# A graph-network kernel's edge MLP: stacked edge attributes, two weight parts side by side, a second addition, and masked register loads

## The reference

```python
edge_input = jnp.concatenate([x[src], x[dst], edge_attr, u[batch[src]]], axis=-1)
h = jax.nn.relu(edge_input @ W1 + b1)
agg = jax.ops.segment_sum(h, dst, num_segments=x.shape[0])
new_input = jnp.concatenate([x, agg, u[batch]], axis=1)
return jax.nn.relu(new_input @ W2 + b2)
```

## Time and profile before

| | us |
|---|---|
| median of 3 executions | 6733.62 |
| lowest, highest | 6725.39, 6737.43 |
| span of the profiled execution | 7388.9 |

### The profile page before, as it was taken

One profiled execution on the slowest core, in us unless ns is written; L12 is line 12 of the kernel. 1 busy time (PEld: TensorE's weight loads), 2 busy tenths in 40 slices (PEclk: granted clock), 3 DMA queues, 4 the chain that ended last, 5 costly groups with the idle time before them and its releaser, 6 DMA issues.

```text
span 7388.9 us, 160613 instructions
## 1 busy us (share of the span) xinstructions
PE 5124.8 (69%) x52214; PEld 4234.4 (57%) x52215; DVE 3236.4 (44%) x5886; ACT 1321.7 (18%) x3390; POOL 2130.6 (29%) x3521
## 2 busy tenths in 40 slices
PE   1999988777777799892655565655565567747665
PEld 1777776666666699892555554554554553323265
DVE  7999888777777611213222222222222231030133
ACT  0122234455555400000000000000000000010010
POOL 1222222222222100002555555555555540000000
PEclk9999999999999989995555555555555558979977
DMA  1011223334343388875222222222222228969755
GB/s 33 24 51 55 79 75 103 131 122 137 123 140 126 117 327 350 341 283 97 60 59 56 60 59 57 59 59 56 59 59 56 60 55 330 418 249 418 319 232 210
DMA packets 427400, 1053.65 MB, mean 143 GB/s; under 512 B 126711, under 2 KB 283713, under 8 KB 398401
## 3 DMA queue, kind: packets, MB, share of 16 engines
q1 hardware_dynamic: 377090, 1000.81, 38.0%
q0 software_dynamic: 50176, 51.48, 3.3%
HBM read 809.69 MB, written 242.41 MB: 142 GB/s over the span
## 4 chain that ended last, share of the span: by engine, by line
PE 45%; another core or an unknown queue 17%; DVE 14%; DMA 8%; issue 7%; ACT 2%; POOLq 2%; ACTq 1%; SPq 1%; DVEq 1%; POOL 0%; PEldq 0%; PEld 0%
PE banks L1504 16%; PE banks L1465 11%; DMA T<-dense_w 8%; PE banks L1428 5%; PE banks L1496 4%; DVE T L816 3%; PE banks L1437 3%; DVE T L823 2%; PE banks L1535 2%; POOLq L342 1%; ACTq L338 1%; PE banks L1423 1%; DVE WORK L905 1%; DVE WORK L893 1%
## 5 line engine op out<-in xcount | busy, mean ns | idle before, releaser
L612 POOL DMA_INDIRECT WORK<-table,idx x1568 | 1498.6, 956 | 2015.5 <-DVE idx L911 872.8
L1504 PE MATMUL banks<-T 128*128 128x125 bf16 (+1 forms) x21696 | 1667.6, 226 | 42.0 <-DVE T L823 7.7
L1504 PEld LDWEIGHTS banks<-T 128*128 128x128 bf16 x21696 | 1441.7, 115 | 337.8 <-DVE T L823 323.8
L816 DVE TENSOR_TENSOR T<-T 128x750 bf16<-128x750 bf16 x1808 | 999.6, 553 | 390.4 <-PE banks L1504 313.1
L569 POOL TENSOR_TENSOR T<-T 128x12 f32 x1816 | 551.2, 304 | 1778.1 <-DVE T L823 1277.2
L823 DVE TENSOR_TENSOR T<-T 128x750 bf16<-128x750 bf16 x1808 | 1000.6, 553 | 62.1
L1496 PE MATMUL banks<-T 128*128 128x250 bf16 x3616 | 709.4, 277 | 362.8 <-DVE T L816 128.7
L1437 PE MATMUL banks<-WORK 128*64 128x128 bf16 x4704 | 633.1, 301 | 416.8 <-issue 410.1
L1465 PE MATMUL banks<-WORK,T 125*128 125x192 bf16 (+1 forms) x10000 | 834.7, 247 | 61.5 <-DVE WORK L955 61.5
L1465 PEld LDWEIGHTS banks<-WORK,T 125*128 125x128 bf16 (+1 forms) x10000 | 832.4, 99 | 63.7 <-issue 47.3
L1428 PE MATMUL banks<-mat,WORK 64*128 64x64 f32 x3136 | 684.6, 376 | 204.5 <-issue 203.0
(11 more groups left out here) (336 smaller groups left out, 3392.7 us busy)
## 6 DMA issues: line engine op xcount, KB each, us to landing
T<-dense_c SPq DMA_DIRECT2D x200, 1562.5 KB, 8.4
T<-dense_w SPq DMA_DIRECT2D x200, 782.0 KB, 10.3
T<-dense_w SPq DMA_DIRECT2D x200, 780.5 KB, 10.4
dense_w<-WORK SPq DMA_DIRECT2D x250, 546.9 KB
WORK<-rel_rows SPq DMA_DIRECT2D x197, 256.0 KB
WORK<-in_eaT SPq DMA_DIRECT2D x196, 256.0 KB
dense_c<-T SPq DMA_DIRECT2D x13, 3125.0 KB, 10.6
dense_c<-ACC SPq DMA_DIRECT2D x12, 3125.0 KB, 10.7
```

Source lines behind the costliest of these rows:

```text
L612: nc.gpsimd.indirect_dma_start(out=g_sb[:, u, c * D:(c + 1) * D], out_offset=None, in_=table, in_offset=bass.IndirectOffsetOnAxis(ap=idx[: ...
L816: V.tensor_tensor(planes[:, v, 0:HOTS].rearrange("p (k n t) -> p k n t", k=3, t=QUAD), iota2[:, 0:LO, :].unsqueeze(1).to_broadcast([P, 3, ...
L1504: last = T.matmul(banks[:, u, to - low // QUAD:to + LO + high // QUAD], keys[:, t, j, :], planes[:, v, first - low:past + high].rearrange( ...
```

## The change

In `z_of` parts one and two of q are moved as one product of 128 columns, so z has two halves per chunk (128 columns of PSUM a chunk, two banks a slab), and part three goes to the first half only. The edge attributes of chunks c and c + 4 are stacked on 128 partitions, and one fp32 product with a block-diagonal 128 x 128 W1c serves two chunks, 4 products a slab and not 8. VectorE adds z in two instructions, the second waiting for the first. The edge attributes come in two transfers of 64 partitions x 512. W1c is set up once by a memset on GpSimd and two copies on ScalarE. Apart from that, every value that `load` fetches into a register, and every value of `loads` whose lower bound isn't negative, is taken through `& MASK` (22 bits) with a register operation of its own.

```diff
+MASK = (1 << 22) - 1
-        ea_sb = WORK[0:D, 3584:5632].rearrange("p (s n) -> p s n", s=2)
+        ea_sb = WORK[:, 3584:4608].rearrange("p (s n) -> p s n", s=2)
+        def slot_of(c):
+            return c % (CHUNKS // 2) * 2 + c // (CHUNKS // 2)
+        z_sums = banks[:, 2:6, :].rearrange("p (s b) n -> p s (b n)", s=2)
...
         def load(eng, of, low, high):
-            return nc.s_assert_within(eng.value_load(of), low, high, ...)
+            return nc.s_assert_within(eng.snap(eng.value_load(of) & MASK), low, high, ...)
...
-            return values
+            if low < 0:
+                return values
+            return [nc.s_assert_within(eng.snap(v & MASK), low, high, ...) for v in values]
...
-                        sp.dma_start(ea_sb[:, u % 2, :], eaT[ds(i * RING + u, 1), :, :].rearrange("a f e -> f (a e)"))\
-                          .then_inc(ea_loaded[u % 2], 16)
+                        for h in range(2):
+                            sp.dma_start(ea_sb[h * D:(h + 1) * D, u % 2, :], eaT[ds(i * RING + u, 1), :, h * HALF_SLAB:(h + 1) * HALF_SLAB].rearrange("a f e -> f (a e)"))\
+                              .then_inc(ea_loaded[u % 2], 16)
...
+            nc.gpsimd.memset(W1c[:], 0.0)
...
-                            V.tensor_tensor(g_sb[:, w, :], banks[:, 2 + v, :], g_sb[:, w, :], ALU.add).then_inc(zsum_ready, 1)
+                            z1, z2 = (z_sums[:, v, :].rearrange("p (c s k f) -> p k s c f", s=2, k=2, f=D)[:, k, :, :, :] for k in range(2))
+                            g = g_sb[:, w, :].rearrange("p (s c f) -> p s c f", s=2, f=D)
+                            V.tensor_tensor(g, z1, g, ALU.add).then_inc(zsum_step, 1)
+                            dve.wait_ge(zsum_step, m + 1)
+                            V.tensor_tensor(g, z2, g, ALU.add).then_inc(zsum_ready, 1)
...
+            for h in range(2):
+                side = slice(h * D, (h + 1) * D)
+                C.activation(W1c[side, side], mat[side, 6 * D:7 * D], ACT.Copy)
...
                     for c in range(CHUNKS):
-                        z, lhsT = banks[:, 2 + v, c * D:(c + 1) * D], hotsT[:, v, c * P:(c + 1) * P]
-                        T.matmul(z, lhsT, QW12[:, ds(at * 2, D)], start=c == 0, stop=False, skip_group_check=True)
-                        T.matmul(z, lhsT, QW12[:, ds(at * 2 + D, D)], start=False, stop=False, skip_group_check=True)
-                        T.matmul(z, lhsT, QW3[:, ds(at, D)], start=False, stop=False, skip_group_check=True)
-                    pe.wait_ge(ea_loaded[v], (r * (SLABS // 2) + i * (RING // 2) + (u // 2 + 1)) * 16)
-                    for c in range(CHUNKS):
-                        last = T.matmul(banks[:, 2 + v, c * D:(c + 1) * D], ea_sb[:, v, c * P:(c + 1) * P], W1c, start=False, stop=c == CHUNKS - 1, skip_group_check=True)
+                        z, lhsT = z_sums[:, v, slot_of(c) * P:(slot_of(c) + 1) * P], hotsT[:, v, c * P:(c + 1) * P]
+                        T.matmul(z, lhsT, QW12[:, ds(at * 2, P)], start=c in (0, 2), stop=False, skip_group_check=True)
+                        T.matmul(z[:, 0:D], lhsT, QW3[:, ds(at, D)], start=False, stop=False, skip_group_check=True)
+                    pe.wait_ge(ea_loaded[v], (r * (SLABS // 2) + i * (RING // 2) + (u // 2 + 1)) * 32)
+                    for c in range(CHUNKS // 2):
+                        last = T.matmul(z_sums[:, v, 2 * c * P:2 * (c + 1) * P].rearrange("p (c h f) -> p h c f", c=2, f=D)[:, 0, :, :], ea_sb[:, v, c * P:(c + 1) * P], W1c[:],
+                                        start=False, stop=c % 2 == 1, skip_group_check=True)
                     last.then_inc(z_ready, 1)
```

More of the change, by code:

```diff
@@ L9 @@
 SLAB = CHUNKS * P
+HALF_SLAB = SLAB // 2
 RING = 4
@@ L221, in gnn_kernel @@
         mat = sb("mat", [P, 12 * D])
-        W1c, W1d, W2b, W2c = (mat[0:D, i * D:(i + 1) * D] for i in (6, 7, 9, 10))
+        W1d, W2b, W2c = (mat[0:D, i * D:(i + 1) * D] for i in (7, 9, 10))
+        W1c = sb("W1c", [P, P])
         W01, W23, WL3 = mat[:, 0:D], mat[:, 2 * D:3 * D], mat[:, 11 * D:12 * D]
@@ L253, in gnn_kernel @@
         z_ready = sem("z_ready")
-        zsum_ready = sem("zsum_ready")
+        zsum_step, zsum_ready = sem("zsum_step"), sem("zsum_ready")
         h_ready = sem("h_ready")
@@ L337, in load @@
         def load(eng, of, low, high):
-            return nc.s_assert_within(eng.value_load(of), low, high, skip_runtime_bounds_check_because="it was worked out within them")
+            return nc.s_assert_within(eng.snap(eng.value_load(of) & MASK), low, high, skip_runtime_bounds_check_because="it was worked out within them")
         def loads(eng, of, low, high):
@@ L343, in loads @@
                                                                  skip_runtime_bounds_check_because="they were worked out within them")
-            return values
+            if low < 0:
+                return values
+            return [nc.s_assert_within(eng.snap(v & MASK), low, high, skip_runtime_bounds_check_because="they were worked out within them") for v in values]
         def bounds_of(eng, g, n):
```

## The result

The changed kernel takes **6766.8 us** (median of 4 runs, 6764.0 to 6767.5), the kernel before 6733.8: a ratio of 1.0056 [1.0041, 1.0070], so slower by 33 us (28 to 47). The direction was forecast, the size (151 us) was not, though 6767 us lies within the range. A later comparison ends on the other side. In it the kernel before took 7378 to 7403 us in its nine runs (median 7386), about the length of the profiled execution shown ahead, and the changed kernel 7321 us: a ratio of 0.991 [0.9897, 0.9924].

A forecast was written before the change was run, and what follows sets the result against it. The edge-MLP pass was taken to run at GpSimd's gathers' pace, the build to wait on TensorE's turns. Terms 0 + 140 + 10 + 1 = +151 us on 6734 gave 6885 us, range 6700 to 6990.

The forecast's parts named there:

- The pass at the gathers' pace: Edge-MLP pass: in plain executions GpSimd's gathers set about 10 us a slab and cover TensorE's and VectorE's changes, 0 us.
- Masks on TensorE: Dense build: five register operations between a turn's load and first product, 0.48 us a turn, +140 us (0 to 246).
- the rule: Dense build: delay ahead of TensorE's first product of a turn reaches VectorE's line 816 one to one, at 292 waits.
- Masks on GpSimd: Dense build: 11 masks a span, mostly covered by the eight quads GpSimd works ahead; +10 us, bounds 0 and 50.
- A: The main forecast, chance 0.58: slower, 6885 us, its own range 6785 to 6990 us.
- C: Rival, chance 0.12: the masks cost nothing, merged into the operations that use the value; no change, 6735 us.
- Edge attributes: Edge-MLP pass, TensorE: 8 records of 128 columns take 2.8 us (1.8 to 3.67), 0.9 us less a slab, covered by gathers.
- Second addition: Edge-MLP pass, VectorE: one more addition and its wait, 0.85 us a slab (0.7 to 1.6), covered by GpSimd's gathers.
- B: Rival, chance 0.16: TensorE's late completions are in plain runs too; fewer instructions save 350 us in the pass, 6535 us.
- D: Rival, chance 0.14: the second addition holds up GpSimd's gathers, adding 55 to 110 us; 6940 to 6995 us.
- The gap of 1.5 us: Sign in the trace after: TensorE's gap at a turn in the build is 1.5 us and not 1.02.
- 450 us of waits for TensorE: Sign in the trace after: line 816's waits for TensorE in the build are near 450 us and not 313.

The follow-up runs named there:

- quick condition: Not one run: sessions in which the unchanged kernel before takes near 6722 to 6734 us; the profile after is from one.
- my layout: Changed kernel with TensorE's masks moved: each loaded value ANDed right behind its load, five ahead of a turn's first product; 7042.5 us, ratio 1.0477.
- late condition: Not one run: sessions in which the unchanged kernel before takes near 7387 us; the profile of before is from one.

## Why the prediction came out as it did

**The pass at the gathers' pace, 0 us: right in the quick condition.** The inference from a profile 655 us over its median (a pass of 1957 us of gathers that the plain runs must have) is borne out by the profile after: 1964.5 us. That this belonged to the profiled execution alone was wrong: it is a condition of whole sessions, and the cover by GpSimd holds in the quick one alone. So the 0 us holds for the condition of the plain runs that it was worked out for. The 0 left out a gain of about 11 us that no term had: a gather is 7 ns shorter in the mean (956 and 949 ns), which is the difference between 1975.7 us of pass with the masks alone and 1964.5.

**Masks on TensorE, +140: the step that failed.** It was "each loaded value gets a register operation, so 5 between the load and the first product". There is one there, and one more of the last group's ahead of the load. The operation's price (0.096 us: load to first product grew from 0.247 to 0.347 us in the median) was right, and the rule held one to one or more; by them the two cost 292 x 0.19 = 56 us, not 140. What they cost in the changed kernel is not measured by itself: the waits for TensorE grew by 8.5 us only, as those for GpSimd grew in their place. Tripling TensorE's masks costs 147 us in the build; the gap grows by 0.37 us in the median, 292 x 0.37 = 107. The rule read from the earlier trace rows was borne out by building my layout, which cost 276 us on top of the changed kernel and 341 on the kernel before. There the price was short too, by four moves that I had only in the upper bound.

**Masks on GpSimd, +10 (0 to 50): mis-sized, and by the same step.** I counted 11 a span, at the load; there are 3053 more in the loops, 1804 of them in the compare. The waits for GpSimd grew by 50 us, and one further mask costs 54. "A slower build widens that cover" was wrong: the waits for GpSimd grew more than those for TensorE.

**Together** 151 was forecast for the build and 65 came. Two errors partly cancelled. In plain runs +33 came; the build's +65 and the pass's -11 would make +54. No trace of the kernel before in the quick condition was taken, so where the other 21 us are is open. The 6767 us lie below A's own range (6785 to 6990), and in the stated one only because that takes in C.

**Edge attributes, 0.9 us less a slab: too small.** At the low clock (0.5 of full) 16 records with the masks alone take 3.67 us and the 8 that take their place in the changed kernel 2.06, so 1.6 us less. From record to record it is 0.217 us with 64 columns and 0.233 with 128, and at full clock 0.115 and 0.123. I had 1.8 us as the lower bound of what is left and took 2.8. The Trainium skill's rule on fast weight loads (TensorE: Matmul & The Clock Gate, section Weight-path perf modes) had pointed at the lower bound, and the trace agrees: 2.06 us lies near it. In the quick condition nothing hangs on it, since the gathers cover it. **Second addition, 0.85 us:** right within its bounds (0.69 and a gap of 0.03), and covered too.

**The rivals.** B, with 0.16, is what happens in the late condition: the changed kernel is faster there. Its mechanism (late completions of TensorE are in the plain runs too) is right for that condition and its size is not: 350 us were worked out, 128 came, 0.65 us a slab. That the count of what TensorE issues decides it was not tested. D's price had the wrong sign: the second addition shortens the gathers. C is excluded by the kernel with the masks alone: 57 us.

Of what I said the trace would show, the 8 records a line, the second addition and the loss in the build came. The gap of 1.5 us, 450 us of waits for TensorE and a last start at 2690 did not (1.21 us, 321.6 us, 2601.2), nor the 0.35 us from record to record at line 1428's place (0.233) and the pass 350 us shorter (128, both late).

## What to carry to other kernels

An operation added to a loaded value was paid where the value is used: look whether that is a loop's compare, and count it once for each iteration. In a loop of two queues that take turns being late, price the change by the next step on each engine, not by the count, for the cost is convex. Before subtracting two profiles, compare each with the median of its own session: 655 us were such a difference here, and the sign of the change hangs on it.

Of the kernels that do all of the work, the one before is the fastest in the quick condition, and the changed one is the fastest of those run in the late condition.

## What the runs showed of the hardware that I had not expected

- A pass bound by GpSimd's gathers got 13 us shorter when VectorE was given 0.69 us more a slab: the place in a gather at which VectorE's instructions fall counts, and 72 of 1568 gathers carry most of it.
- Loads of six values into TensorE's registers took 1.47 us in the median, of five 0.58, of eleven 1.99.
- TensorE has a condition in which, in the edge-MLP pass, it issues single instructions up to 2.7 us late and its signal behind a product rises up to 28 us late, through a whole session, on a chip that had been free of it in another. The build takes the same time in both.
